# Layer 1 heads moved one or two slots earlier, with other PSUM banks, near the end of a fused two-layer transformer block

## What is computed

```python
x = L0_attn_query                                   # (8, 256, 256)
xn = layernorm(x)
x = x + attn0(xn, ...) + ffn0(xn, ...)               # 16 heads of 128, causal; fp8 GELU ffn
xn = layernorm(x)
x = x + attn1(xn, ...) + ffn1(xn, ...)               # 16 heads of 16; SiLU ffn between Hadamard transforms

# attn0: softmax((q k^T) / sqrt(128) - 1e10 * (1 - causal)) v, then w_o
# attn1: softmax((q k^T) / 16) v, then Wo
# ffn1:  silu(x_gate) * x_up, 1024 hidden features, then W_down
```

## Time and profile before

| | us |
|---|---|
| median of 3 runs | 956.28 (956.0 to 956.56) |
| the profiled execution | 956.0 |
| its span | 954.1 |
| PE busy | 891.1 (93%) |
| DVE busy | 748.6 (78%) |
| ACT busy | 678.5 (71%) |
| POOL busy | 355.8 (37%) |

### The profile page before, as it was taken

The page is one execution under the profiler, slowest core; times in us unless marked ns, Lnnn a source line. Parts: engine busy times, 40 slices in busy tenths (PEclk is TensorE's granted clock), DMA queues, the critical chain, the costliest instruction groups (busy, mean ns, idle before and its releaser), DMA issues.

```text
span 954.1 us, 22854 instructions
## 1 busy us (share of the span) xinstructions
PE 891.1 (93%) x8016; PEld 719.3 (75%) x8016; DVE 748.6 (78%) x2128; ACT 678.5 (71%) x1997; POOL 355.8 (37%) x653
## 2 busy tenths in 40 slices
PE   4876989899999999999999999999999999997897
PEld 2334767677888888888888888888888888876675
DVE  6787677667888888878887888788878888887776
ACT  4788786456776777777777776777677776775664
POOL 4503456423343333333333333233433343334342
PEclk9899999999999999999999999999999999999999
DMA  9343360002000200020002000110001000200000
GB/s 292 110 155 105 100 211 2 2 15 71 1 1 13 62 15 10 2 68 6 24 2 61 14 23 1 40 36 24 1 25 50 24 2 3 56 4 21 1 13 12
DMA packets 46879, 39.96 MB, mean 42 GB/s; under 512 B 4400, under 2 KB 42032, under 8 KB 46512
## 3 DMA queue, kind: packets, MB, share of 16 engines
q1 hardware_dynamic: 46768, 38.52, 13.1%
HBM read 30.11 MB, written 8.39 MB: 40 GB/s over the span
## 4 chain that ended last, share of the span: by engine, by line
PE 70%; DVE 13%; ACT 7%; issue 3%; POOL 1%; ACTq 0%; DVEq 0%; POOLq 0%
PE ps L824 37%; PE ps L942 7%; PE ps L870 6%; PE ps L845 4%; PE ps L1062 4%; PE ps L1042 4%; ACT arena L1168 3%; DVE arena L818 3%; DVE arena L817 2%; ACT arena L813 2%; DVE arena L1328 2%; PE ps L1073 2%; PE ps L905 2%; PE ps L954 2%; PE ps L1044 2%
## 5 line engine op out<-in xcount | busy, mean ns | idle before, releaser
L818 DVE SCALAR_TENSOR_TENSOR arena<-ps,bqk,arena 128x256 bf16<-128x256 f32 x416 | 187.5, 480 | 70.5 <-ACT arena L813 70.5
L813 ACT ACTIVATE arena<-ps,bqk 128x256 bf16<-128x256 f32 x416 | 177.4, 462 | 69.5 <-PE ps L1044 55.9
L817 DVE TENSOR_TENSOR arena<-ps,arena 128x512 bf16<-128x512 f32 (+1 forms) x336 | 203.4, 633 | 23.8 <-ACT arena L812 23.7
L824 PE MATMUL ps<-arena,wqkv 128*128 128x256 bf16 x1728 | 212.5, 273 | 0.0
L1168 ACT ACTIVATE arena<-arena,nb 128x128 f32<-128x128 f32 (+1 forms) x256 | 114.4, 448 | 125.2 <-DVE nb L1328 125.1
L1563 POOL TENSOR_SCALAR arena<-arena,rc 128x128 f32<-128x128 f32 (+1 forms) x256 | 105.5, 425 | 256.1 <-DVE rc L1357 255.9
L1570 POOL TENSOR_SCALAR arena<-arena,rc 128x256 f32<-128x256 f32 x254 | 118.2, 478 | 203.7 <-DVE rc L1361 203.7
L812 ACT ACTIVATE arena<-ps 128x512 bf16<-128x512 f32 (+1 forms) x336 | 175.3, 558 | 25.9 <-PE ps L824 15.5
L824 PEld LDWEIGHTS ps<-arena,wqkv 128*128 128x128 bf16 x1728 | 169.3, 98 | 21.1
L1168 ACT ACTIVATE arena<-ps,nb 128x256 f32<-128x256 f32 x256 | 119.9, 483 | 19.3 <-DVE nb L1335 19.2
L824 PE MATMUL ps<-arena 128*128 128x128 bf16 (+2 forms) x864 | 97.4, 248 | 12.1 <-DVE arena L817 7.4
(11 more groups left out here) (116 smaller groups left out, 1287.5 us busy)
## 6 DMA issues: line engine op xcount, KB each, us to landing
scratch_qk<-arena SPq DMA_DIRECT2D x28, 128.0 KB, 1.9
arena<-scratch_qk SPq DMA_DIRECT2D x84, 32.0 KB, 1.8
arena<-scratch_qk SPq DMA_DIRECT2D x42, 64.0 KB, 2.5
arena<-in_x SPq DMA_DIRECT2D x4, 512.0 KB, 9.8
arena<-in_w_gating SPq DMA_DIRECT2D x4, 512.0 KB, 8.7
arena<-in_w_q SPq DMA_DIRECT2D x4, 512.0 KB, 4.6
arena<-in_w_k SPq DMA_DIRECT2D x4, 512.0 KB, 6.0
arena<-in_w_v SPq DMA_DIRECT2D x2, 1024.0 KB, 6.7
```

Of the source, the lines that this page charges most:

```text
L813: return nc.scalar.activation(out, in_, ACT.Identity, bias=bias)
L817: return nc.vector.tensor_tensor(out, in_, hi, ALU.subtract)
L818: return nc.vector.scalar_tensor_tensor(out=out, in0=in_, scalar=bias, in1=hi, op0=ALU.add, op1=ALU.subtract)
L824: last = nc.tensor.matmul(out, lhsT, rhs, start=(n == 0), stop=(n == len(steps) - 1))
```

## The change

It changes tables and the waits that follow from them; no arithmetic is added or taken away.

- `head_slot` of batch 6: its heads stand by twos in slots 124, 125 and 126, one in 127, by twos in 128 to 131 and one in 132. Slot 133 has none. Quads and output projections of batch 6 move with them (`quad_slot` from 129, 132, 133, 135 to 127, 130, 133, 134; `out_slot` from 130, 133, 134, 136 to 128, 134, 134, 135), and the batch's result from slot 137 to 136.
- `turn1_bank`: the transposes of second heads whose turn is below slot 128 (heads 97, 99 and 101) go to `BK_QK`, the bank of `proj_qk0`. `proj_qk0` of a later slot then waits for their `p1_low` (a wait that the code had already, for a list that was empty).
- `piece_bank`: q, k and v of batch 7 go to `BK_S`, `BK_O` and `BK_X`, one each, where they had `BK_VU`, `BK_X` and again `BK_VU`. They wait for the last use of those banks, among it `p1_low` of head 110, and no longer for the feed-forward part or for each other.
- Batch 6's result stands at the end of its slot on DVE, not at its head.

```diff
@@
             if b == LASTB - 1:
-                return start1(b) + 12 + (0, 1, 2, 3, 4, 4, 5, 5, 6, 6, 7, 7, 8, 8, 9, 9)[h]
+                return start1(b) + 12 + (0, 0, 1, 1, 2, 2, 3, 4, 4, 5, 5, 6, 6, 7, 7, 8)[h]
...
-                return start1(b) + (17, 20, 21, 23)[q]
+                return start1(b) + (15, 18, 21, 22)[q]
...
-                return start1(b) + (18, 21, 22, 24)[q]
+                return start1(b) + (16, 22, 22, 23)[q]
...
         def piece_bank(n):
             b, w = divmod(n, 3)
-            return BK_M if b < LASTB else (BK_VU, BK_X, BK_VU)[w]
+            return BK_M if b < LASTB else (BK_S, BK_O, BK_X)[w]
...
                 if second(n):
-                    return BK_S if n < LASTB * H1 - 1 else BK_X
+                    return BK_QK if head_slot(n) + 1 < NG0 else BK_S
...
-                elif bank == BK_X:
-                    pe.wait_ge(qkv1_lo, 3 * LASTB + 2)
+                elif bank == BK_X or bank == BK_O and n >= LASTB * H1:
+                    pe.wait_ge(qkv1_lo, 3 * B)
                 elif bank == BK_O:
                     pe.wait_ge(o0_lo, min(slot - 3, NG0))
+                    if slot >= piece_slot(3 * LASTB):
+                        pe.wait_ge(qkv1_lo, 3 * LASTB + 2)
...
                 else:
-                    pe.wait_ge(h1, KH * LASTB)
-                    upto(pe, qkv1_lo, 3 * LASTB + 1 if w == 2 else 0)
+                    pe.wait_ge(p0_lo, NG0)
+                    pe.wait_ge(o0_lo, NG0)
+                    pe.wait_ge(p1_lo, 1 + max(m for m in range(LASTB * H1) if head_slot(m) + 1 < piece_slot(n)))
                     pe.wait_ge(x1_done, B)
...
-                if b == LASTB and m == 0:
-                    pe.wait_ge(qkv1_lo, 3 * B)
...
                 for b in y_in[s]:
-                    if b == LASTB:
-                        result(b)
+                    result(b)
```

## The result

| | before | after |
|---|---|---|
| median, run side by side (4 runs each) | 956.42 us (956.0 to 957.16) | 965.83 us (964.99 to 966.11) |
| the profiled execution | 956.0 | 964.64 |
| its span | 954.1 | 962.7 |

The changed kernel is slower by the ratio 1.0096 [1.0079, 1.0113], that is +9.4 us where +5.3 was forecast, and outside the range given (957.0 to 964.5). The direction was right and the size was not. The two profiled executions differ by 8.6 us, and it is these 8.6 us that the trace can be asked about. A ratio that differs from 1.0000 beyond its interval is a difference here; all of them are under 1%.

The account below looks back on a forecast made before the run. PE was taken to bound the slots the heads enter, with DVE as long as PE already. Terms 7.6 + 0.2 - 2.2 - 0.3 = +5.3 us on 956.0 gave 961.3 (961.6 for the median), range 957.0 to 964.5.

Parts of the forecast that it names:

- the loss in slots 124 to 127: Second heads' waits (3 x 1.76), their low parts (3 x 0.60) and the BK_M wait (0.7) lengthen DVE's chain: +7.6 us.
- the term for slots 132 and 133: Projections start 0.8 us later, then run with fewer waits and less work: -2.2 us, bounds -3.3 to 0.
- the term for slots 128 to 131: Path otherwise unchanged; an o1_high enters slot 128 ahead of p1_high, of which about 0.2 us shows: +0.2 us (0 to 0.5).
- PE covered by DVE: Slots 124 to 127: PE's added 2.5 us and proj_qk0's new wait for p1_low are hidden behind DVE's pace.
- One of the signs: If the forecast is right, PE waits for DVE ahead of turn0 in each of slots 125 to 128.
- Rival 1: DVE and ACT keep up, PE stays the bound in slots 124 to 127: -0.9 us, 955.4; chance 0.14.
- rival 2: DVE's added work lands (4.05 us) but the waits are hidden by PE running ahead: +1.8, 958.1; chance 0.18.
- the rival that contains it: Rival 3: part of slots 126 to 133 falls to the lower clock level, +2 to +4 us on top; chance 0.14.
- The last 55 us: Slot 134 to the end: two heads' transposes leave PE and one output projection enters: -0.3 us.
- Rival 3: Lower clock in part of slots 126 to 133, PE's work ends behind DVE: +2 to +4 us, 963.5 to 965.5; chance 0.14.

Follow-up runs that it names:

- defer_after: The changed kernel with second heads' exponential on ACT behind the gate's tanh and reciprocal on DVE behind hidden, below slot 128 only; ratio 1.0053 to before.
- fill_after: The changed kernel plus 60 idle matmuls, output never read, where TensorE waits in slots 129 to 133; ratio 1.0054 to before, median 964.03 us.
- defer_tables: The changed kernel with the old q, k, v banks and every second head's exponential and reciprocal deferred, in all slots; ratio 1.0013 to before.
- after_again: The changed kernel itself, unchanged, as a control on another chip; ratio 1.0082 to before.
- dose_one: The kernel before with only the first moved pair (heads 96 and 97 in slot 124), q, k, v banks as before; ratio 1.0018 to before.
- tables_only: The changed kernel with the old banks for q, k, v and their waits put back; ratio 1.0069 to before.
- dose_two: The kernel before with only the first two moved pairs (two heads each in slots 124 and 125), q, k, v banks as before; ratio 1.0046 to before.
- seam_only: The kernel before with only the new banks for q, k, v of batch 7 and their waits, all slots as before; ratio 1.0000 to before.
- before_again: The kernel before itself, unchanged, as a control on another chip; ratio 0.9993 to before.

## Why the prediction was right or wrong

In short: the loss in slots 124 to 127 was priced rightly. The step that failed is the term for slots 132 and 133, -2.2 us, with +1.0 measured. Behind it stands the term for slots 128 to 131, +0.2 us, with +2.0 measured. In the sum both put the lower clock at nothing, and it was 1.4 + 2.1 us; another 1.1 us in slots 132 and 133 are the waits behind the new banks.

**Second heads in slots 124 to 127: right.** 3 x 1.76 + 3 x 0.60 + 0.7 - 0.15 = 7.6 us were forecast, +7.9 measured, and the parts hold singly: 2.31 and 2.30 for one head (2.36), 0.80 for `BK_M` (0.7). The rows of a place where two heads stood already were the right price list. The slots last 7.13, 8.02 and 9.02 us, where about 7.1, 8.0 and 8.8 were named. Slot 127 lasts 6.77 where the terms give 6.04 + 0.60 = 6.64.

**PE covered by DVE: right in the main.** The new matmuls in these slots show nowhere in DVE's length. The new wait of `proj_qk0` for `p1_low` shows a little: in slot 127 it held PE for 1.09 us, and DVE then waited 0.68 us for q and k where it had waited 0.55, the 0.13 us that slot 127 is longer than its terms. One of the signs came out otherwise. PE waited for DVE ahead of `turn0` in slots 125 and 128 only (0.98 and 0.22 us, and not the 1.09 that I had let stand in slot 128); in slot 126 it waited ahead of the scores of head 101 and in slot 127 ahead of that projection. Where the wait stands is another place, and DVE's pace is what PE is held to all the same. Rival 1 (PE stays the bound, 955.4) is refuted. So is rival 2: `defer_after` removed the waits and left the work, and 1.7 us went. What stands behind the wait was not foreseen: PE's quad and its 1.94 us for `BK_M`, and then DVE's 0.68 us for PE.

**Slots 128 to 131: the term of +0.2 us was mis-sized**, +2.0 measured. 0.6 is the step as I described it and at full clock (25.68 in `fill_after` against 25.04); slot 128 holds it, where an output's evacuation stands ahead of `max_1` and DVE is idle for 1.01 us:

```profile
867.53 0.48 DVE L818 SCALAR_TENSOR_TENSOR arena<-ps,bv,arena 128x256 bf16<-128x256 f32 x1 [1.01 <-ACT arena L813]
```

The other 1.4 us are the clock in slot 130. I had looked for the clock's risk in how busy the entered slots would be. What changed instead were the slots that the work left: the quad that had stood in 129 is gone from there, and PE's wait ahead of slot 130's `turn1` grew from 1.83 to 2.49 us. From slot 129's first `turn1` to slot 130's it is 7.30 us in both kernels, so DVE's chain sets that stretch and PE only waits longer in it. Whether the longer wait is why the clock fell is open: it fell behind a wait of this length in two of six executions, of five kernels.

**Slots 132 and 133: this term failed**, -2.2 forecast and +1.0 measured, by two causes. The projections start 7.13 us after the transposes and not 6.78: `p1_low` of head 110 starts where I had it (899.50, which is 6.18 us behind them), and PE starts 0.95 us after it where I took 0.6. And behind them 6.58 us at full clock stood against my 5.8, of which 0.4 is a wait of 0.62 us for k's low part that was sized at 0.2:

```profile
907.29 0.63 PE L872 MATMUL ps<-ident,arena 128*128 128x128 f32 x4 [0.62 <-DVE arena L818]
```

The rest of that 0.8 is small: 0.16 for the end of the last projection, 0.13 for head 111's transposes, 0.1 for `down`. That makes 13.71 instead of 12.64, 1.1 us. The new tables with the old banks had 12.48 in `defer_tables`, nearly at full clock behind the start of the projections, so this miss lies with the new banks: I had put their exchange at nearly nothing, 0.8 us of wait for 0.73. The other 2.1 us are the clock, 15.84 against 13.71. I had it in the bounds of this term ("0 if the clock of 0.71 lasts through the projections for some 2 us"), and gave the rival that contains it a chance of 0.14. The clock had fallen in slot 132 of before already, and it is low there in every execution without idle matmuls. I took the favourable end of my own bounds without a reason.

**The last 55 us**: -0.3 forecast, -1.6 measured, of which some 1.3 are the clock that did not fall at the end (6.67 and 5.33 us for the same 50 matmuls). Nothing in the change aims at this. It came in after, `after_again`, `defer_after` and `dose_one`, and not in `tables_only`, `fill_after` or `dose_two`, and I have no rule for it.

The sum closes: 5.3 forecast, +0.3 in slots 124 to 127, +0.4 and +1.4 in 128 to 131, +1.1 and +2.1 in 132 and 133, -1.3 at the end, -0.7 ahead of slot 124 make 8.6 us. Net of its fall and its gift at the end the clock is +2.2 us of it. Rival 3 put +2 to +4 us on top of the forecast and 963.5 to 965.5 (961.3 and the same additions make 963.3 to 965.3); the profiled execution had 964.64. So it is the forecast's mechanism with rival 3's cost on top, though not by rival 3's way. It had PE's slowed work in the entered slots end behind DVE. Where the clock did fall there, in `fill_after`, that cost 0.27 us. That the size agrees is luck in part, since the 1.3 us at the end came back. The median is 1.2 us above that execution. The executions of after have a mean granted clock of 0.986 at 964.64 and 964.99 us and of 0.982 to 0.984 at 965.71 to 966.11, so the clock goes with this too; where it fell in them no trace says.

**The rule on banks.** The Trainium skill (Perfetto Trace Analysis, Optimizing Tensor Performance) would rotate banks between the three projections. The trace agrees that the wait between the groups goes (0.73 us in before, 0.62 in `tables_only`). What comes for it was under-sized: 1.41 us ahead of them in `seam_only` and 1.25 in after, and the projections start 1.6 and 1.5 us later than with the old banks and the same tables. Against before the start was forecast 0.8 us later, and in after it is 1.15 us later (7.13 and 5.98). The trace of `seam_only` puts the exchange at 0.8 to 1.2 us; its ratio of 1.0000 confirms neither that nor a gain.

## What to carry to other kernels

Price work that moves into a slot by the whole in-order stretch it opens on every engine, read where such a pair already stands, and not by its busy time: here 0.60 us of work came with 1.76 us of shift, of which 1.01 were idle time for another engine's result, on an engine that the page calls 78% busy. Put other work ahead of an instruction that would wait so, and look for the next chain: that order alone won 0.3%, where moving heads lost 0.8 to 1.0%. Ask also of the slots that lose work how long TensorE's waits become there. The clock may fall behind such a wait, and the matmuls that follow pay for it where PE is the bound.

## What was not expected of the hardware

The granted clock at one place of one kernel is not the same in each execution: 0.71 in slot 132 of before and 0.56 in `before_again`, with 14.84 and 16.03 us for two slots. After the same wait of 2.13 us at the end it was 0.77 in before and 1.00 in after, and after the same 2.49 us it fell in after and not in `tables_only`. Matmuls whose result nobody reads seem to pay for themselves: with sixty of them the ratio of the changed kernel is 1.0054, without them 1.0082 or 1.0096, and with 42 the deferred one has 0.9940 for 0.9971. These are ratios from different chips, and the intervals of 1.0082 and 1.0054 overlap.

Left open: what decides whether the clock falls in slot 130, at the end and in the first 106 us.
